# Graph network in four layers on one core: four and five gather buffers, one VectorE increment per group of operations, frames per five chunks

## The chip, the cores and the metric

One core of a Trainium2 chip. The metric is the device time of one execution in microseconds (us), as the median of three runs. Engines: PE is TensorE, DVE is VectorE, ACT is ScalarE, POOL is GpSimd, SP is SyncE. A semaphore is a counter in hardware that instructions increment when they finish and that others wait on.

## The reference

12,500 nodes with 32 features and 400,000 edges, sorted by their target `dst`. Each of four layers gathers the features of the source node of every edge, makes a message of them and of the edge's attributes, adds the messages up by target, and is followed by a residual and a layer norm:

```python
x = _layernorm(x + _L0_gnn_ref(x, edge_index, edge_weight1, edge_attr_3, edge_attr_5, L0_gnn_W), axis=-1)
x = _layernorm(x + _L1_gnn_ref(x, edge_attr_2, L1_gnn_weight, edge_index), axis=-1)
x = _layernorm(x + _L2_gnn_ref(x, edge_index, edge_attr_2, L2_gnn_g, L2_gnn_mu, ...), axis=-1)
x = _layernorm(x + _L3_gnn_ref(x, edge_weight, edge_attr_3, edge_index, ...), axis=-1)
```

The first layer multiplies the gathered, transformed features with products of spherical harmonics `sh0`, `sh1`, `sh2` (one, three and five attributes per edge). The third takes three 32-wide blocks of `x[src] @ g`, weights them with three Gaussians of the edge's two attributes and adds them:

```python
diff = edge_vectors[:, None, :] - mu[None, :, :]
gauss = jnp.exp(-0.5 * jnp.sum(diff * diff / (EPS + sigma[None] ** 2), axis=-1))
msg = jnp.sum((x[src] @ g).reshape(e, k, cout) * gauss[:, :, None], axis=1)
```

## The kernel before, in words

The edges lie on 128 partitions with 3,125 each. An edge stage works in 125 **chunks** of T = 25 edges per partition. For each chunk SyncE loads the source indices and the attributes, GpSimd issues 25 indirect DMAs (each gathers one row per partition from a table in DRAM: 512 bytes in the first layer, 384 in the third), VectorE makes the messages and runs a scan along the edges (the mask from ScalarE restarts it at each new target), and ScalarE turns the scan's result and stores it. After the stage the rows at the ends of the runs are fetched. The first and the third layer use the same frame (`vector_edges`, `scalar_edges`, `gpsimd_edges`, `sync_edges`, with `layer` 0 or 2); layers two and four have code of their own, which stays as it is.

There are three gather buffers, `L.gb[k % 3]`, and each engine runs a hardware loop of 25 bodies of five chunks (BODY = 5). Since five is no multiple of three, a table says which chunk used a buffer last:

```python
BEFORE3 = {0: (3, 1), 1: (4, 1), 2: (2, 1), 3: (0, 0), 4: (1, 0)}
```

Chunk 0 of a body waits for chunk 3 of the body before, that is two chunks back, and chunk 1 for chunk 4, two back as well; chunk 2 waits for the one five back; 3 and 4 for the one three back. SyncE and GpSimd both wait on VectorE's counter `dv` for the last product that reads the buffer (`mk[layer, "g", b_]`), SyncE before it loads the indices (line 2075), GpSimd before its gathers (line 1912).

VectorE increments `dv` with every instruction, 29 times per chunk in the first layer (27 in the body function and 2 for the copy and the scan behind it) and 27 in the third (25 + 2), and `after(e)` (line 392) makes it wait until all its own increments have arrived, ahead of each step that reads what the step before wrote. The first layer's steps per chunk are: five one-hots (L584, for a histogram of the sources on TensorE), three copies (L870 to L872), six small operations (L875 to L879), two more (L881, L882), nine products (L891 to L898), two reductions (L901, L902), a copy (L1164) and the scan (L1169). The third layer's are the direction frames of 25 columns (L913 to L944, stored to `Y_d` for the fourth layer), the Gaussians (L955 to L961), the product (L966), the reduction (L971), and copy and scan. ScalarE takes a square root and an exponential for each chunk (L1391, L1393).

In the first layer SyncE issues six DMAs per chunk: indices (L2075), three attributes (L2078), and two stores that fill scratch areas (L2079, L2080). In the third it issues four: indices, two attributes (L2082, L2085) and the store of the frames (L2089).

## Time and profile before

| | |
|---|---|
| median of 3 runs | 22449.03 us (22440.92 to 22450.41) |
| the profiled execution: span | 22477.8 us; its time outside the span isn't given, and the span lies 28.8 us above the median |
| first layer's edge stage | 170 to 4642 us |
| third layer's edge stage | 11500 to 15920 us |
| busy over the span | PE 33%, PEld 24%, DVE 56%, ACT 16%, POOL 57% |
| busy in the first layer's stage | DVE 2792 us, POOL 2952 us of 4472 us |
| busy in the third layer's stage | DVE 1528 us, POOL 2953 us of 4420 us |

How to read it: GpSimd counts as busy only while it works on an indirect DMA (0.94 us each), not in the 0.30 us between two, so its busy share in a stage without any pause would be some 75%. Waiting instructions and DMA issues aren't busy time. In a row of the timeline the brackets give how long the engine was idle before it, and what ended that; "issue" and "remote" name no instruction.

### The profile page before, as it was taken

To read this page: it belongs to the slowest core of one execution; us is meant where nothing else is said; L and a number is where in the kernel's file an instruction comes from. 1 tells how busy PE (TensorE), PEld (TensorE's weight loads), DVE (VectorE), ACT (ScalarE), POOL (GpSimd) and SP (SyncE) were. 2 spreads that over 40 slices of the span, in tenths; PEclk is the share of its full clock that TensorE was granted. 3 is DMA by queue.
4 is the path that set the end of the run, shared out by engine and by line. 5 is a ranking of instruction groups with operands and counts; after the bars stand their busy time and mean duration, and the time that the engine had idled before them with its cause. 6 is when DMAs were issued, how large, how long until landed. Compare 5 with 4: busy or idle time off the path is not lost. (4 is left out here: it accounts for less than half of the span.)

```text
span 22477.8 us, 146858 instructions
## 1 busy us (share of the span) xinstructions
PE 7373.1 (33%) x33487; PEld 5470.9 (24%) x33487; DVE 12681.8 (56%) x18038; ACT 3608.5 (16%) x5762; POOL 12798.1 (57%) x13715
## 2 busy tenths in 40 slices
PE   1111011114444444444420000000166666666664
PEld 0000000003333333333310000000155555555553
DVE  5666666646666666666753333333366666666665
ACT  0000000001111111111531111111111111111111
POOL 6666666655555555555656666666644444444444
PEclk9755555556666666666755555555588888888887
DMA  3222222210000000000322222222111111111111
GB/s 92 86 86 86 85 83 86 87 34 19 19 18 18 18 19 19 18 18 18 128 90 52 52 52 52 52 52 52 36 38 35 37 35 35 37 35 35 37 35 30
DMA packets 787591, 1077.91 MB, mean 48 GB/s; under 512 B 412503, under 2 KB 554765, under 8 KB 774494
## 3 DMA queue, kind: packets, MB, share of 16 engines
q0 software_dynamic: 417376, 477.82, 9.8%
q1 hardware_dynamic: 294051, 398.16, 6.4%
q10 hardware_dynamic: 75736, 197.70, 2.4%
q14 instruction: 340, 2.79, 0.0%
q8 instruction: 88, 1.44, 0.0%
HBM read 684.92 MB, written 389.48 MB: 48 GB/s over the span
## 5 line engine op out<-in xcount | busy, mean ns | idle before, releaser
L1912 POOL DMA_INDIRECT s_arena<-d_t,s_arena x6250 | 5901.2, 944 | 2983.8 <-issue 2482.7
L1884 POOL DMA_INDIRECT s_arena<-d_t,s_arena x3125 | 2958.8, 947 | 3193.9 <-DVE s_arena L1033 1127.9
L1845 POOL DMA_INDIRECT d_pay<-s_arena x3125 | 3025.9, 968 | 2938.8 <-DVE s_arena L717 1469.3
L1699 PE MATMUL psall<-s_w2r,s_arena 128*128 128x384 f32 x4750 | 2070.4, 572 | 1635.6 <-DVE s_arena L1033 844.5
L1593 PE MATMUL psall<-s_arena 128*128 128x500 bf16 x1875 | 986.3, 553 | 4661.7 <-DVE s_arena L584 2352.5
L1619 PE MATMUL psall<-s_arena 128*128 128x128 f32 x6250 | 1338.7, 377 | 1877.6 <-ACT s_arena L1339 1560.6
L1699 PEld LDWEIGHTS psall<-s_w2r,s_arena 128*128 128x128 f32 x4750 | 1445.0, 319 | 1993.2 <-DVE s_arena L1033 904.9
L1619 PEld LDWEIGHTS psall<-s_arena 128*128 128x128 f32 x6250 | 1149.8, 274 | 2180.6 <-issue 1210.6
L1030 DVE TENSOR_TENSOR s_arena<-psall,s_arena 128x512 f32<-128x512 f32 x1000 | 788.9, 789 | 1554.6 <-remote 1367.5
L1593 PEld LDWEIGHTS psall<-s_arena 128*128 128x128 bf16 x1875 | 219.4, 117 | 5234.3 <-DVE s_arena L584 2495.5
L1785 PE MATMUL psall<-s_tails,s_mfix 128*128 128x32 f32 x6 | 1.9, 411 | 4445.4 <-DVE s_tails L1177 4445.4
L1042 DVE TENSOR_REDUCE s_arena<-s_arena 128x64 f32<-128x1024 f32 x1000 | 1401.5, 1412 | 0.2 <-issue 0.2
L901 DVE TENSOR_REDUCE s_arena<-s_arena 128x600 f32<-128x4200 f32 x125 | 1027.2, 8218 | 552.2 <-remote 519.1
L1507 ACT ACTIVATE s_arena<-s_arena 128x800 f32<-128x800 f32 x250 | 428.8, 1715 | 5470.3 <-issue 3357.9
L1339 ACT ACTIVATE s_arena<-psall 128x512 f32<-128x512 f32 x875 | 482.4, 551 | 4870.9 <-remote 2623.7
L708 DVE TENSOR_TENSOR s_arena<-psall,s_arena 128x512 f32<-128x512 f32 x875 | 551.0, 630 | 1048.8 <-remote 939.2
L1610 PE MATMUL psall<-s_ident,s_arena 128*128 128x128 f32 x3125 | 718.7, 369 | 1274.2 <-DVE s_arena L685 1274.2
L1785 PEld LDWEIGHTS psall<-s_tails,s_mfix 128*128 128x128 f32 x6 | 1.5, 313 | 4446.7 <-DVE s_tails L1177 4446.7
L697 DVE TENSOR_TENSOR s_arena<-s_arena,psall 128x625 f32<-128x625 bf16 x625 | 503.5, 806 | 1008.3 <-remote 706.5
L584 DVE TENSOR_TENSOR s_arena<-s_arena,psall 128x625 bf16<-128x625 f32 x1250 | 944.9, 800 | 0.4 <-DVE s_arena L1151 0.4
L1610 PEld LDWEIGHTS psall<-s_ident,s_arena 128*128 128x128 f32 x3125 | 551.7, 196 | 1297.3 <-issue 1297.3
L685 DVE TENSOR_TENSOR s_arena<-s_arena,psall 128x1536 f32<-128x1536 f32 x250 | 781.6, 3168 | 4.4
(296 smaller groups left out, 16815.9 us busy)
## 6 DMA issues: line engine op xcount, KB each, us to landing
s_arena<-d_t,s_arena POOLq DMA_INDIRECT x9375
d_scan<-s_arena ACTq DMA_DIRECT2D x375, 400.0 KB
s_arena<-d_ew SPq DMA_DIRECT2D x126, 800.0 KB, 6.4
s_arena<-d_pay SPq DMA_DIRECT2D x33, 1650.0 KB, 6.9
d_inj<-s_agg SPq DMA_DIRECT2D x125, 400.0 KB
s_arena<-d_inj SPq DMA_DIRECT2D x125, 400.0 KB
d_pay<-s_arena POOLq DMA_INDIRECT x3125
d_pay<-s_agg SPq DMA_DIRECT2D x100, 429.0 KB
```

Source lines behind the costliest of these rows:

```text
L584: return e.tensor_tensor(O[sl], h5[:, :, bass.ds(n, 1)].to_broadcast([P, 5, 125]), iob, ALU.is_equal)
L685: up(e.tensor_tensor(xb[:, t0:t1], so_[:, t0:t1].unsqueeze(2).to_broadcast([P, t1 - t0, 4, 32]), tv[:, t0:t1].unsqueeze(3).to_broadcast([P ...
L901: e.tensor_reduce(S[:, :, 8:32], w7.rearrange("p m t c -> p t c m"), AX.X, ALU.add).then_inc(dv.up(), 1)
L1030: e.tensor_tensor(pr[:, :, 0:256].rearrange("p t (b v) -> p t b v", v=16), Rg[:, :, 0:256].rearrange("p t (b v) -> p t b v", v=16), L3.G[s ...
L1042: e.tensor_reduce(L3.sums[s2][:, t0:t0 + n].rearrange("p t c -> p (t c)"), prod(g).rearrange("p t (b v) -> p (t b) v", v=16), AX.X, ALU.ad ...
L1593: e.matmul(R5s[:, 0:4], lhsT, rhs[:, 0:4], start=start, stop=True, skip_group_check=True)
L1610: m = e.transpose(ps[6][:, 128 * t:128 * t + 128], S1.xb[:, 128 * (t0 + t):128 * (t0 + t) + 128], ident[:, :])
L1619: m = e.matmul(ps[2 + yb][:, 128 * t:128 * t + 128], S1.xT[yb][:, 128 * t:128 * t + 128], S1.wt, start=True, stop=True)
L1699: m = e.matmul(ps[BANK[g] + t][:, 0:384], hv_[:, :, t0 + t], L3.w2v if g in ONPE else w2r[:, :], start=True, stop=True)
L1845: e.indirect_dma_start(pay_d, bass.IndirectOffsetOnAxis(ap=S1.adr[s4][:, t:t + 1], axis=0), S1.pay[s4][:, 33 * t:33 * t + 33], None).then_ ...
L1884: e.indirect_dma_start(L3.gb[s][:, t], None, T3_d, bass.IndirectOffsetOnAxis(ap=L3.idx[s][:, t:t + 1], axis=0)).then_inc(sem(f"g3_{s}"), 16)
L1912: e.indirect_dma_start(L.gb[s][:, t * L.CW:(t + 1) * L.CW], None, L.tab, bass.IndirectOffsetOnAxis(ap=L.idx[s][:, t:t + 1], axis=0)).then_ ...
```

## The change

*First layer.* Four gather, attribute and index buffers instead of three. Chunk 0 stands ahead of the loop, then 31 bodies of four chunks, so each chunk reuses the buffer of the chunk four before it. VectorE increments `dv` five times per chunk: when the attributes are copied ("ready"), the small operations done ("turned", "oh"), the products done ("g"), the sums done ("S"). It waits on its own count five times. The scan of a chunk comes first in the next chunk. The one-hots come in groups of three and two among the small operations, and TensorE's count of them goes up once per chunk. ScalarE's mask has two PSUM buffers.

*Third layer.* Five gather, index, row and scan buffers, and still bodies of five. VectorE increments `dv` three times per chunk. The frames and the Gaussians are computed for the five chunks of the next body at once (125 columns), in twelve steps of which one is put behind the product, the reduction and the scan of each chunk but the fifth; the first body's are done ahead of the loop. Square root and exponential come once per body. SyncE loads the attributes and stores the frames once per body, and loads each index list five chunks ahead.

The rest of the kernel is the same. The core of the diff (removed functions are in the listing above):

```diff
-BODY = 5
-IT = TP // (T * BODY)
+B2 = 5
+IT2 = TP // (T * B2)
...
-            L.gb = [cv(T * L.CW) for _ in range(3)]
-            L.idx = [cv(T, U32) for _ in range(3)]
...
+        L0.gb = [cv(T * 128) for _ in range(3)]
+        L0.idx = [cv(T, U32) for _ in range(3)]
+        L0.at = [cv(T * 9) for _ in range(3)]
...
+        cv = Carve(21400)
+        L0.gb.append(cv(T * 128))
+        L0.at.append(cv(T * 9))
+        L0.idx.append(cv(T, U32))
...
+        TB = T * B2
+        L2.CW = 96
+        L2.gb = [cv(T * 96) for _ in range(B2)]
+        L2.idx = [cv(T, U32) for _ in range(B2)]
...
+        L2.dirs, L2.at, L2.YS = cv(TB * 3), cv(TB * 2), cv(TB * 9)
+        L2.DF, L2.GS, L2.SQ, L2.n2 = part(cv(TB * 6), 0, 6, TB), part(cv(TB * 3), 0, 3, TB), part(cv(TB * 3), 0, 3, TB), part(cv(TB), 0, 1, TB)
...
+        PER0 = 5
+        AT0 = {"ready": 1, "turned": 2, "oh": 3, "g": 4, "S": 5}
+        def v0(c, name):
+            return c * PER0 + (mk["base0"] + AT0[name])
+        def vector_scan0(e, c, s2):
+            e.wait_ge(dv.h, v0(c, "S"))
+            e.wait_ge(sem("am0"), c + 1)
+            e.wait_ge(sem("rowc0"), c + 1)
+            return e.tensor_tensor_scan(L0.so[s2], mr[s2], L0.si[s2], 0.0, ALU.mult, ALU.add)
...
+        def vector_chunk0(e, c, i, k):
+            s, s2 = k % 4, k % 2
...
+            if i is not None:
+                vector_scan0(e, c - 1, 1 - s2)
+            e.wait_ge(sem(f"at0_{s}"), nth4(0 if i is None else i, k) * 48)
+            e.tensor_copy(a0, tv(0, 1))
+            e.tensor_copy(s1x[:, :, 0:3], tv(1, 3))
+            e.tensor_copy(s1x[:, :, 3:5], tv(1, 3)[:, :, 0:2]).then_inc(dv.up(), 1)
+            e.wait_ge(sem("cnt_pe"), c + 1)
+            for q in range(3):
+                onehot(e, c * 5 + q, q)
+            e.wait_ge(dv.h, v0(c, "ready"))
+            e.tensor_copy(L0.siv[s2][:, :, 0:1], L0.sov[1 - s2][:, :, T:T + 1])
+            e.tensor_scalar(sn, s1x[:, :, 2:5], -1.0, None, ALU.mult)
             for o0, st_, f in ((2, 4, 0), (1, 2, 1), (5, 2, 3)):
...
+                e.tensor_scalar(Q[:, :, o0:o0 + st_ + 1:st_], a2[:, :, f:f + 1].to_broadcast([P, T, 2]), QA, None, ALU.mult)
+            e.tensor_scalar(Q[:, :, 4:5], a2[:, :, 2:3], QC, None, ALU.mult)
             e.tensor_scalar(bm, a2[:, :, 2:3], -QB, None, ALU.mult).then_inc(dv.up(), 1)
...
+            for q in range(3, 5):
+                onehot(e, c * 5 + q, q)
+            e.wait_ge(dv.h, v0(c, "turned"))
+            e.scalar_tensor_tensor(out=Q[:, :, 0:1], in0=a2[:, :, 4:5], scalar=-QA, in1=bm, op0=ALU.mult, op1=ALU.add)
             e.scalar_tensor_tensor(out=Q[:, :, 8:9], in0=a2[:, :, 4:5], scalar=QA, in1=bm, op0=ALU.mult, op1=ALU.add).then_inc(dv.up(), 1)
...
+            e.wait_ge(sem(f"g_{s}"), nth4(0 if i is None else i, k) * 400)
+            e.tensor_tensor(w7[:, 0], A1_, a0.to_broadcast([P, T, 24]), ALU.mult)
+            e.tensor_tensor(wu(1), b3(A2_, 3), bm2(a1, 8), ALU.mult)
+            e.tensor_tensor(wu(2), A4_[:, :, :, 2:5], bm2(s1x[:, :, 1:4], 8), ALU.mult)
+            e.tensor_tensor(wu(3), A4_[:, :, :, 1:4], bm2(sn, 8), ALU.mult)
+            e.tensor_tensor(w4[:, :, :, 0], g0[:, :, 0:8], a0.to_broadcast([P, T, 8]), ALU.mult)
+            e.tensor_tensor(w4[:, :, :, 1:4], A3_, bm2(a1, 8), ALU.mult)
+            e.wait_ge(dv.h, v0(c, "oh"))
             for j in range(3):
...
+                m = e.tensor_tensor(wu(4 + j), A5_[:, :, :, j:j + 1].to_broadcast([P, T, 8, 3]), bm2(Q[:, :, 3 * j:3 * j + 3], 8), ALU.mult)
+            m.then_inc(dv.up(), 1)
+            e.wait_ge(dv.h, v0(c, "g"))
+            e.tensor_reduce(S[:, :, 8:32], w7.rearrange("p m t c -> p t c m"), AX.X, ALU.add)
             e.tensor_reduce(S[:, :, 0:8], w4, AX.X, ALU.add).then_inc(dv.up(), 1)
...
+        PER2L = 3 * B2
+        def of0(k):
+            return (32, 31, 31, 31, 0)[k]
+        def vl2(i, k, n):
+            return i * PER2L + (mk["base2l"] + 3 * k + n)
...
+            if ph == 0:
+                e.wait_ge(sem("dr2"), 16 * step + 16)
+                e.tensor_tensor(SQ, a3, a3, ALU.mult)
+                e.wait_ge(sem("at2"), 16 * step + 16)
+                return e.tensor_tensor(DV, bm2(a2, 3), mug[:, :].rearrange("p (k d) -> p k d", k=3).unsqueeze(1).to_broadcast([P, TB, 3, 2]), ALU.subtract)
+            if ph == 1:
+                e.tensor_tensor(DF, DF, DF, ALU.mult)
+                return e.tensor_reduce(n2, SQ, AX.X, ALU.add)
+            if ph == 2:
+                return e.tensor_tensor(DF, DF, sgg[:, :].unsqueeze(1).to_broadcast([P, TB, 6]), ALU.mult)
+            if ph == 3:
+                return e.tensor_reduce(L2.GS, DV, AX.X, ALU.add)
+            if ph == 4:
+                e.wait_ge(sem("ac_n2"), step + 1)
+                return e.reciprocal(n2, n2)
+            if ph == 5:
+                e.wait_ge(sem("yst"), 16 * step + 16)
+                e.tensor_tensor(n_[:, :, 0:2], a3[:, :, 1:3], n2.to_broadcast([P, TB, 2]), ALU.mult)
+                return e.tensor_tensor(n_[:, :, 2:3], a3[:, :, 0:1], n2, ALU.mult)
+            if ph == 6:
...
+        def vector_chunk2l(e, i, k, last):
...
+            prev = L2.sov[(k - 1) % B2]
+            step = i + 1
+            e.wait_ge(dv.h, vl2(i, k, 0))
+            if k == 0:
+                e.wait_ge(sem("ac_gs"), step)
+            e.wait_ge(sem(f"g_{k}"), i * 400 + (400 + 400 * of0(k)))
+            m = e.tensor_tensor(
+                L2.work.rearrange("p (q c) -> p q c", c=32), g0.rearrange("p t (q c) -> p (t q) c", c=32),
+                L2.GSP[:, k * T:k * T + T].rearrange("p t (q o) -> p (t q) o", o=1).to_broadcast([P, 3 * T, 32]), ALU.mult)
+            if not last and k < 4:
+                m = vector_frames(e, i, 3 * k, step)
+            m.then_inc(dv.up(), 1)
+            e.wait_ge(dv.h, vl2(i, k, 1))
+            e.tensor_copy(L2.siv[:, :, 0:1], prev[:, :, T:T + 1])
+            m = e.tensor_reduce(L2.sit, L2.work.rearrange("p (t q c) -> p t c q", t=T, q=3), AX.X, ALU.add)
+            if not last and k < 4:
+                m = vector_frames(e, i, 3 * k + 1, step)
+            m.then_inc(dv.up(), 1)
+            e.wait_ge(dv.h, vl2(i, k, 2))
+            e.wait_ge(sem("am2"), c + 1)
+            e.wait_ge(sem("rowc2"), c + 1)
+            m = e.tensor_tensor_scan(L2.so[k], mr[0], L2.si, 0.0, ALU.mult, ALU.add)
+            if not last and k < 4:
+                m = vector_frames(e, i, 3 * k + 2, step)
+            m.then_inc(dv.up(), 1)
+        def vector_edges2(e):
+            e.memset(mrv[0][:, :, 0:1], 0.0).then_inc(dv.up(), 1)
...
+            mk["first2l"] = dv.n
+            for ph in range(12):
+                if ph:
+                    after(e)
+                vector_frames(e, 0, ph, 0).then_inc(dv.up(), 1)
+            mk["base2l"] = dv.n
...
+        def scalar_chunk2l(e, i, k, last):
+            c = i * B2 + k
+            e.wait_ge(dv.h, vl2(i, k, 0))
+            scalar_mask(e, c, 0, 2)
+            if not last and k == 1:
+                e.wait_ge(dv.h, vl2(i, 0, 2))
+                e.activation(L2.n2, L2.n2, ACT.Sqrt).then_inc(sem("ac_n2"), 1)
+            if not last and k == 4:
+                e.wait_ge(dv.h, vl2(i, 4, 1))
+                e.activation(L2.GSP, L2.GS, ACT.Exp, scale=-0.5).then_inc(sem("ac_gs"), 1)
+            e.wait_ge(dv.h, vl2(i, k, 3))
+            e.wait_ge(sem(f"rowd2_{k}"), i * 16 + 16)
+            e.activation(L2.row[k].rearrange("p (t f) -> p t f", t=T), L2.sov[k][:, :, 1:T + 1].rearrange("p f t -> p t f"), ACT.Copy).then_inc(sem("rowc2"), 1)
...
+        def gpsimd_chunk0(e, c, i, k):
+            s = k % 4
+            e.wait_ge(sem(f"ix_{s}"), nth4(0 if i is None else i, k) * 16)
+            held(e)
+            e.wait_ge(dv.h, v0(c - 4, "g"))
+            held(e)
+            for t in range(T):
...
+                    e.wait_ge(sem(f"ix_{k}"), i * 16 + (16 + 16 * of0(k)))
...
+                    e.wait_ge(dv.h, vl2(i - 1, k, 1))
...
+        def sync_chunk0(e, c, i, k):
+            s = k % 4
+            e.wait_ge(dv.h, v0(c - 4, "g"))
+            e.sem_inc(idle2, 1)
+            e.dma_start(L0.idx[s].bitcast(I32), src_v[:, bass.ds(c * T, T)]).then_inc(sem(f"ix_{s}"), 16)
+            for o, w_, a_ in ((0, 1, ew1), (1, 3, ea3), (4, 5, ea5)):
+                e.dma_start(L0.at[s][:, o * T:(o + w_) * T], a_.rearrange("(p t) d -> p (t d)", p=P)[:, bass.ds(c * (T * w_), T * w_)]).then_inc(sem(f"at0_{s}"), 16)
+            if i is None:
+                lo_, n = 0, 14
+            else:
+                lo_, n = i * (106 * 33) + (14 + 27 * (k - 1) - (k == 4)) * 33, 26 + (k < 3)
+            e.dma_start(pay_d.rearrange("(p t) c -> p (t c)", p=P)[:, bass.ds(lo_, 33 * n)], agg[:, 0:33 * n]).then_inc(sem("fill_p"), 16)
+            e.dma_start(inj_d[0:E, :].rearrange("(p t) f -> p (t f)", p=P)[:, bass.ds(c * 800, 800)], agg[:, 924:1724]).then_inc(sem("fill_z"), 16)
...
+            with e.Fori(0, IT2 - 2) as i:
+                for k in range(B2):
+                    sync_after2(e, i, k, 1)
+                    sync_index2(e, i + 1, k)
+                    if k == 2:
+                        sync_attr2(e, i + 2)
+                    if k == 4:
+                        e.dma_start(Y_d[:, bass.ds((i + 1) * (TB * 9), TB * 9)], L2.YS).then_inc(sem("yst"), 16)
```

Three places where the order of the instructions changes. VectorE, first layer, in the loop, from the attribute copies on; `m_dv` is its own counter, `m_at0_1` the attributes, `m_cnt_pe` TensorE's count. Before:

```order
L870 COPY psall<-s_arena 128x25 [waits m_at0_1,m_dv]
L871 COPY psall<-s_arena 128x25x3
L872 COPY psall<-s_arena 128x25x2
L392 REGISTER_ALU
L875 TENSOR_SCALAR psall<-psall 128x75 [waits m_dv]
L877 TENSOR_SCALAR psall<-s_arena 128x25x2 x3
L878 TENSOR_SCALAR psall<-s_arena 128x25
L879 TENSOR_SCALAR s_arena<-s_arena 128x25
L392 REGISTER_ALU
L881 SCALAR_TENSOR_TENSOR psall<-s_arena 128x25 [waits m_dv]
L882 SCALAR_TENSOR_TENSOR psall<-s_arena 128x25
L392 REGISTER_ALU
```

After:

```order
L870 COPY s_arena<-s_arena 128x32 [waits m_dv]
L871 TENSOR_SCALAR psall<-psall 128x75
L873 TENSOR_SCALAR psall<-s_arena 128x25x2 x3
L874 TENSOR_SCALAR psall<-s_arena 128x25
L875 TENSOR_SCALAR s_arena<-s_arena 128x25
L564 ISA
L564 TENSOR_TENSOR s_arena<-s_arena,psall 128x5x125
L564 ISA
L564 TENSOR_TENSOR s_arena<-s_arena,psall 128x5x125
L879 REGISTER_ALU
L880 SCALAR_TENSOR_TENSOR psall<-s_arena 128x25 [waits m_dv]
L881 SCALAR_TENSOR_TENSOR psall<-s_arena 128x25
```

Before, every copy, operation and product here carries an increment; in the new order only L875 and L881 do (and L864, the last attribute copy, some rows earlier), and two one-hots stand between the small operations and the wait of L880.

VectorE, third layer, from the Gaussians of a chunk to its scan; `m_g2_1` and `m_g_1` are gathers, `m_ac_gs` and `m_ac_n2` ScalarE's results. Before:

```order
L955 TENSOR_TENSOR s_arena<-s_arena,s_mug 128x150 [waits m_at2_1]
L392 REGISTER_ALU
L957 TENSOR_TENSOR s_arena<-s_arena 128x150 [waits m_dv]
L392 REGISTER_ALU
L959 TENSOR_TENSOR s_arena<-s_arena,s_sgg 128x150 [waits m_dv]
L392 REGISTER_ALU
L961 TENSOR_REDUCE s_arena<-s_arena 128x75 [waits m_dv]
L966 TENSOR_TENSOR s_arena<-s_arena,psall 128x2400 [waits m_g2_1,m_ac_gs]
L392 REGISTER_ALU
L971 TENSOR_REDUCE s_arena<-s_arena 128x25x32 [waits m_dv]
L392 REGISTER_ALU
L1164 COPY s_arena<-s_arena 128x32 [waits m_dv]
```

After:

```order
L992 TENSOR_TENSOR s_arena<-s_arena,psall 128x2400 [waits m_g_1]
L953 TENSOR_REDUCE s_arena<-s_arena 128x375
L999 REGISTER_ALU
L1000 COPY s_arena<-s_arena 128x32 [waits m_dv]
L1001 TENSOR_REDUCE s_arena<-s_arena 128x25x32
L955 REGISTER_ALU
L956 RECIPROCAL s_arena<-s_arena 128x125 [waits m_ac_n2]
L1006 REGISTER_ALU
L1007 REGISTER_ALU [waits m_dv]
L1009 SCALAR_TENSOR_TENSOR s_arena<-psall,s_arena 128x832 [waits m_rowc2,m_am2]
L959 TENSOR_TENSOR s_arena<-s_arena 128x125x2 [waits m_yst]
L960 TENSOR_TENSOR s_arena<-s_arena 128x125
```

The product no longer waits for Gaussians of its own chunk; behind product, reduction and scan one step of the next body's frames stands each time.

SyncE, third layer, one chunk before:

```order
L2075 ISA [waits m_dv]
L2075 DMA s_arena<-in_src 128x25
L2082 ISA
L2082 DMA s_arena<-in_edge_attr 128x50
L2083 REGISTER_ALU
L2085 ISA [waits m_dv]
L2085 DMA s_arena<-in_edge_attr 128x75
L2087 ISA
L2089 ISA [waits m_dv]
L2089 DMA d_y<-s_arena 128x225
```

After, chunks 1 to 3 of a body:

```order
L2158 ISA [waits m_dv]
L2158 DMA s_arena<-in_src 128x25
L2162 REGISTER_ALU
L2158 ISA [waits m_dv]
L2158 DMA s_arena<-in_src 128x25
L2153 ISA
L2153 DMA s_arena<-in_edge_attr 128x250
L2154 ISA
L2154 DMA s_arena<-in_edge_attr 128x375
L2162 REGISTER_ALU
L2158 ISA [waits m_dv]
L2158 DMA s_arena<-in_src 128x25
```

Of four DMAs per chunk one is left, and the attributes of five chunks are loaded together in the body's third chunk.

## Rows read from the trace of the kernel before

**Rows 1.** The page: its first line and its part 1 (busy us, share, instructions).

```profile
span 22477.8 us, 146858 instructions
PE 7373.1 (33%) x33487; PEld 5470.9 (24%) x33487; DVE 12681.8 (56%) x18038; ACT 3608.5 (16%) x5762; POOL 12798.1 (57%) x13715
```

**Rows 2.** Busy time by stage: us, PE, PEld, DVE, ACT, POOL, clock, DMA, GB/s.

```profile
170.00:4642.00 4472.00, 441.31 (x1250) 81.67 (x1250) 2791.96 (x3672) 319.75 (x250) 2952.15 (x3129) 0.58 0.30 85
...
11500.00:15920.00 4420.00, 4.86 (x28) 3.29 (x28) 1528.35 (x3395) 733.23 (x793) 2952.71 (x3125) 0.50 0.22 52
```

**Rows 3.** Line L1912, 170 to 4660 us: duration min/median/max, first and last start.

```profile
L1912 POOL DMA_INDIRECT s_arena<-d_t,s_arena x3125: 938/944/967, 180.0 to 4587.5; - x196
```

**Rows 4.** The same line from 11500 to 16000 us.

```profile
L1912 POOL DMA_INDIRECT s_arena<-d_t,s_arena x3125: 938/944/1172, 11517.0 to 15904.7; - x196
```

**Rows 5.** Timeline of GpSimd, 2069 to 2140 us: start, duration, engine, idle before.

```profile
2108.12 0.94 POOL L1912 DMA_INDIRECT s_arena<-d_t,s_arena  x1 [0.30 <-issue]
2134.66 0.94 POOL L1912 DMA_INDIRECT s_arena<-d_t,s_arena  x1 [25.59 <-DMA s_arena<-in_src]
```

**Rows 6.** VectorE's line groups, 170 to 4660 us: busy, mean ns, idle before.

```profile
L901 DVE TENSOR_REDUCE s_arena<-s_arena 128x600 f32<-128x4200 f32 x125 | 1027.2, 8218 | 552.2 <-remote 519.1 <-issue 29.5 <-DVE s_arena L898 2.8
...
L1169 DVE TENSOR_TENSOR_SCAN s_arena<-psall,s_arena 128x832 f32<-128x832 f32 x125 | 236.3, 1891 | 29.0 <-issue 21.8 <-DVE s_arena L1164 7.2
...
L891 DVE TENSOR_TENSOR s_arena<-s_arena,psall 128x600 f32<-128x600 f32 x125 | 97.5, 780 | 276.7 <-remote 212.3 <-issue 61.4 <-DVE psall L882 1.9
...
L875 DVE TENSOR_SCALAR psall<-psall 128x75 f32<-128x75 f32 x125 | 30.6, 245 | 183.1 <-remote 127.4 <-issue 52.0 <-DVE psall L872 2.2
...
L881 DVE SCALAR_TENSOR_TENSOR psall<-s_arena 128x25 f32<-128x25 f32 x125 | 25.8, 206 | 611.0 <-remote 479.9 <-issue 130.2
```

**Rows 7.** Timeline of all engines, 2042 to 2066 us.

```profile
2042.36 0.20 DVE L881 SCALAR_TENSOR_TENSOR psall<-s_arena 128x25 f32<-128x25 f32 x1 [6.93 <-remote]
...
2045.16 0.78 DVE L891 TENSOR_TENSOR s_arena<-s_arena,psall 128x600 f32<-128x600 f32 x1 [2.49 <-remote]
2045.81 0.70 SPq L2079 DMA_DIRECT2D d_pay<-s_agg  x1
...
2050.33 0.77 DVE L898 TENSOR_TENSOR s_arena<-s_arena,psall 128x600 f32<-128x600 f32 x1
...
2057.06 8.22 DVE L901 TENSOR_REDUCE s_arena<-s_arena 128x600 f32<-128x4200 f32 x1 [5.96 <-remote]
```

**Rows 8.** Timeline of VectorE, the first layer's last chunk.

```profile
4618.11 3.64 DVE L584 TENSOR_TENSOR s_arena<-s_arena,psall 128x625 bf16<-128x625 f32 x5
...
4623.40 0.78 DVE L891 TENSOR_TENSOR s_arena<-s_arena,psall 128x600 f32<-128x600 f32 x1
...
4629.38 8.22 DVE L901 TENSOR_REDUCE s_arena<-s_arena 128x600 f32<-128x4200 f32 x1
...
4638.91 1.89 DVE L1169 TENSOR_TENSOR_SCAN s_arena<-psall,s_arena 128x832 f32<-128x832 f32 x1 [0.19 <-DVE s_arena L1164]
```

**Rows 9.** VectorE's line groups, 11500 to 16000 us.

```profile
L966 DVE TENSOR_TENSOR s_arena<-s_arena,psall 128x2400 f32<-128x2400 f32 x125 | 332.0, 2656 | 626.9 <-DMA s_arena<-d_t,s_arena 534.2 <-ACT psall L1393 79.4 <-issue 13.2
...
L957 DVE TENSOR_TENSOR s_arena<-s_arena 128x150 f32<-128x150 f32 x125 | 39.6, 317 | 845.6 <-remote 575.1 <-issue 267.7 <-DVE s_arena L955 2.5
```

**Rows 10.** Timeline of all engines, 176 to 186 us.

```profile
177.15 0.40 SPq L2075 DMA_DIRECT2D s_arena<-in_src  x1
...
180.03 0.95 POOL L1912 DMA_INDIRECT s_arena<-d_t,s_arena  x1 [5.47 <-DMA s_arena<-in_src]
...
184.90 0.08 DVE L557 MEMSET s_cst<- 128x1 f32 x4
```

**Rows 11.** Timeline of all engines, 15880 to 15935 us.

```profile
15907.26 2.66 DVE L966 TENSOR_TENSOR s_arena<-s_arena,psall 128x2400 f32<-128x2400 f32 x1 [1.97 <-DMA s_arena<-d_t,s_arena]
```

**Rows 12.** SyncE's waits, 170 to 4660 us: total us, times, longest.

```profile
SPq L2074 <- remote: 1024.0, 44, 55.3
SPq L2074 <- DVE s_arena L898: 330.3, 8, 49.8
```

503 lines of the change are left out of this document (208 added, 295 removed).

## The prediction

> **What bounds the kernel now.** I read the page first, then each engine's busy time by stage, then the queue of gathers, then VectorE's line groups and a piece of the timeline. On the page no engine is busy for more than 57% of the span [rows 1], so the limit differs by stage. The change touches two: the first layer's edge loop (170 to 4642 us) and the third layer's (11500 to 15920 us), each 125 chunks of 25 gathers [rows 2]. The other 13,400 us run the same instructions as before, and I cost them at nothing.
>
> In the first layer the gathers start at 180.0 us and the last of the 3,125 at 4587.5 us [rows 3]; in the third from 11517.0 to 15904.7 us [rows 4]. A gather takes 0.94 us and the next starts 0.30 us behind it, and then one comes after 25.59 us, behind an index load [rows 5]. I took the step between every two neighbours. In the first layer the median is 1.249 us, no step inside a chunk is over 1.273 us, and the excess over 3,124 equal steps is 4407.5 - 3902 = 505 us, nearly all of it in the 24 steps where a body of five ends (21.7 us each). In the third it is 4387.7 - 3902 = 486 us, spread over most chunk boundaries (4 to 9 us). So GpSimd's queue has a floor of 3902 us in each stage, and something makes it wait for 991 us in all.
>
> What it waits for is VectorE. In the first layer VectorE is busy 2792 us [rows 2], 22.3 us per chunk, and idle 552 + 611 + 277 + 183 = 1623 us before four lines [rows 6]: together 4415 of the 4461 us. It is never starved of data there (except for the first chunk); it waits for its own increments. The group L891 to L898, nine instructions with an increment each, ends at 2051.1, but L901, which needs the ninth, starts at 2057.06; meanwhile SyncE's DMA issues take 0.70 us each instead of the 0.40 us of the stage's first [rows 7, 10]. From L891 to L901 that is 11.9 us for nine increments, 1.3 us each; L881 and L882, two increments, take 2.8 us. In the last chunk, when SyncE and the gathers are through, the same nine instructions take 5.98 us and the whole chunk, 4618.11 to 4640.80, takes 22.7 us [rows 8]. So beside SyncE's work an increment costs up to 1.4 us, and the 29 of a chunk lengthen it from 22.7 us to 35.7 in the mean (4461 / 125).
>
> With three buffers and a body of five, chunk 0 of a body reuses buffer 0, last used two chunks earlier instead of three. There GpSimd has to wait for the slow VectorE, then for SyncE, then for the index load; this is the 21.7 us. The third layer has the same arrangement and 27 increments per chunk, with much longer waits in its chain of small operations [rows 9].
>
> **The change, part by part.** *Buffers.* With four buffers and bodies of four (five and five), every chunk waits for the one four (five) before it. That leaves at least three chunks of gathers, 94 us, for one chunk of VectorE and one of SyncE, so if VectorE needs under 31.2 us per chunk (25 x 1.249), GpSimd never waits.
>
> *Increments, first layer.* 29 per chunk become 5. The chunk keeps its operations and so its 22.3 us of busy time. VectorE waits for itself five times; at the worst seen, 1.4 us behind a single increment, that is 7 us, so 22.3 to 29.3 us. Two of the waits stand behind three and two one-hots (0.73 us each), and the wait for "oh" behind six products, so I take two exposed waits: 22.3 + 2.8 = 25.1 us. All of it is below 31.2 us, so it costs nothing on the path. **Term 1: -505 us.**
>
> *The end of the first layer.* Today VectorE is behind: from the start of the last gather to the end of the last scan 4640.8 - 4587.5 = 53.3 us pass. Afterwards it is idle when the last gather lands. The third layer shows that distance now: 15904.7 to L966 at 15907.26, 2.6 us [rows 11]. Then come 17.4 us from L891 to the end of the scan [rows 8], and up to two waits of 1.4 us (I take one): 21.4 us. **Term 2: -32 us.**
>
> *The start of the first layer.* SyncE's first index load now waits for VectorE's count to reach 16 below its value at the loop. Before it was 33 below, passed at 176.9 us; counted back along the instructions, 16 below falls on the last of the four memsets of L557, at 185.0 us [rows 10]. The first gather, at 180.03, follows. **Term 3: +8 us.**
>
> *Third layer.* 27 increments become 3 per chunk. The direction and Gaussian work is done once per five chunks on 125 columns instead of 25, spread over twelve of the fifteen steps of a body. VectorE's 12.2 us per chunk (1528 / 125 [rows 2]) can only shrink, since fewer instructions move the same elements; with three waits of 1.4 us it is under 17 us. ScalarE's square root and exponential come once per body. The first body's twelve steps run before VectorE's first product, while the first 31 us of gathers run; even at two waits each they delay no buffer among five. **Term 4: -486 us**, and one memset less ahead of the barrier, -0.8 us. The tail stays: already now VectorE waits for the last gather there.
>
> *SyncE.* In the first layer it waits 1024 + 330 us for VectorE's count [rows 12], so it works some 3,100 us, 24.8 us per chunk, beside those increments. Six DMAs per chunk stay, with 24 increments fewer to compete with: 24.8 us is the upper bound and below 31.2. In the third layer, eight DMAs per body replace twenty. The larger loads and the larger Y store (128x1125) lie more than a chunk ahead of their use. Cost nothing; without that cover a body would pay one load, 2 to 3 us.
>
> *GpSimd.* Same gathers. A step of 1.249 us is the sum's main price. Its bounds are rows of busy time: 938 ns at least and 1172 ns at most, against a median of 944 [rows 4].
>
> Here a rule speaks against the change. What the row shows is L901 starting 5.96 us behind nine increments, and no wait in the last chunk [rows 7, 8]. The Trainium skill, VectorE: DVE Perf Modes, section "The DRAIN you can't avoid", says that eight copies with a semaphore after each took the same time as with one only after the last, and its rules say to minimize the count of operations, not of semaphores. By that rule the last chunk agrees and the middle of the stage does not; if it held, term 1 would be zero. 
>
> **Sum:** -505 - 32 + 8 - 486 - 1 = -1016 us against a span of 22477.8. The page gives no other time of this execution than its span, which is 28.8 us above the median of the runs, 22449.0; I subtract from the median: **21433 us**, 4.5% faster.
>
> **The rivals.**
> *B: the waits do not follow the number of increments.* If VectorE's 13.2 us of waiting per chunk (1652 / 125, the four lines and the scan's 29 us [rows 6]) stayed in the first layer, a chunk would be 35.5 us and VectorE would set the pace: terms 1 and 2 are lost. 22449 + 8 - 487 = 21970 us. For it: a wait is also two register instructions. Against: 2, 6 and 9 increments wait 2.5, 6.9 and 6.0 us behind their instructions. If instead each exposed wait cost 3.3 us, the present mean (1652 / 500), a chunk would be 31 to 33 us, and the time up to 21433 + 125 x 1.8 = 21660 us. Chance 0.06 for both.
> *C: GpSimd still pauses at some body boundaries*, because SyncE comes to an index load late behind its fills. A mean of a quarter of today's pause per body, 5.4 us x 31, and half the third layer's excess: +167 + 243 = 21840 us. Against: the slack of several chunks. Chance 0.05.
> *D, slower: the gathers themselves slow down.* GpSimd now pauses 11% of both stages; without pauses, and with VectorE's work no longer broken up by waits, each gather would have to exceed (4407.5 + 4387.7) / 6248 = 1.408 us for the kernel to lose. If each took the longest seen, 1172 instead of 944 ns, the step would be 1.477 us: 6248 x 0.069 = +431 us, less the 25 us of terms 2 and 3: 22855 us. Against: inside the first layer's chunks no step moves by 2% while VectorE is busy 62% of the time, and in the third 99 of 100 steps are below 1.303 us. The Trainium skill, SBUF — State Buffer, section on the doors into SBUF ("The 'DVE blocks DMA' trap"), has such a mechanism: a 2-port copy on VectorE keeps GpSimd from writing descriptors. By that rule copies should show as late gathers; in this trace they do not. Chance 0.03.
> *E: no difference* (within 0.2%, 45 us, about what a measurement of this kernel can tell): the gains and a partial D cancel. Chance 0.02.
>
> **How the numbers follow.** The forecast has 0.84. Its own range: a step of 1.244 us, the smallest seen, would give 31 us more; five exposed waits change only the tail, by 4 us; a load exposed once per body would cost 56 bodies x 2.5 = 140 us. So 21400 to 21570; the mild form of B lies half inside it. A fifth or less is left out, so it is the range of the whole. The forecast, B and C are all faster: faster 0.95, same 0.02, slower 0.03.
>
> **What would show it.** Gathers of the first layer from 188 to 4090 us, with no pause over 2 us; those of the third spanning 3902 us; steps of 1.249 us. VectorE idle in both stages ahead of the first product (L890, L992), waiting for a gather, and at most 1.4 us ahead of the reductions; its first-layer busy time still near 2790 us, in the third below 1528. SyncE waiting more than before. The first layer's last scan some 21 us behind the last gather. The prediction is wrong if VectorE's idle time in the first layer lies before the reductions instead (B), if pauses of GpSimd follow an index load (C), or if its step is above 1.26 us (D).

## The result, and the profile after

| | before | after |
|---|---|---|
| median of 5 runs | 22450.41 us (22440.92 to 22453.89) | 22371.12 us (22360.98 to 22384.42) |
| ratio, 95% interval | | 0.9965, 0.9955 to 0.9976 |
| span of the profiled execution | 22477.8 us | 22369.0 us |

The change is worth 79 us (0.35%), not 1016; the time is 801 us above the range's upper end. Three views answer to [rows 1 to 4]: the page's first part; the two stages by windows (us, then PE, PEld, DVE, ACT, POOL busy, clock, DMA share, GB/s); the two lines of gathers (duration ns min/median/max, first to last start):

```profile
PE 7326.9 (33%) x33487; PEld 5554.2 (25%) x33487; DVE 12331.2 (55%) x15713; ACT 3280.0 (15%) x5336; POOL 13220.2 (59%) x13715
```

```profile
170.00:4642.00 4472.00, 350.77 (x1250) 144.16 (x1250) 2787.07 (x3669) 317.63 (x249) 2995.38 (x3128) 0.54 0.30 85
11430.00:15820.00 4390.00, 14.76 (x95) 10.27 (x91) 1192.29 (x1098) 411.02 (x402) 3321.54 (x3126) 0.50 0.22 53
```

```profile
L1957 POOL DMA_INDIRECT s_arena<-d_t,s_arena x3125: 938/945/1803, 202.2 to 4570.8; - x196
...
L1979 POOL DMA_INDIRECT s_arena<-d_t,s_arena x3125: 940/946/2245, 11454.7 to 15800.7; - x196
```

From first to last start, the gathers take 4368.6 us in the first layer and 4346.0 us in the third, against 4407.5 and 4387.7 before: 81 us less instead of 991.

The two layers miss 3902 us in different ways, which the starts of the gathers show. In the first layer GpSimd still pauses: 56 steps, all at the start of a chunk, are longer than 3.2 us, and they hold 417 of the 467 us over 3902; the steps inside chunks hold 48. In the third it never pauses so long, but its busy time rose from 2953 to 3322 us: 1208 of 3124 steps are longer than 1.3 us, 731 of them between 1.38 and 1.42.

Not all of the 79 us need come from the two loops that were changed. In this pair of traces the first layer gives nothing to the total: its gathers start 22.2 us later, its last scan comes 72.7 us behind its last gather instead of 53.3, and the second layer's gathers start at 4971.7 us against 4968.9. The second layer's gathers, whose code is the same, take 5856.0 us against 5918.1, which is 62 of the 109 us between the spans; the pair on one chip below has no such difference.

VectorE's line groups of the first layer (busy, mean ns, idle before) answer to [rows 6]:

```profile
L901 DVE TENSOR_REDUCE s_arena<-s_arena 128x600 f32<-128x4200 f32 x125 | 1027.2, 8218 | 775.5 <-remote 678.6 <-issue 96.2
L564 DVE TENSOR_TENSOR s_arena<-s_arena,psall 128x625 bf16<-128x625 f32 x625 | 473.6, 803 | 132.8 <-issue 132.4
L898 DVE TENSOR_TENSOR s_arena<-s_arena,psall 128x600 f32<-128x600 f32 x375 | 284.6, 775 | 203.1 <-issue 170.9 <-remote 32.1
...
L890 DVE TENSOR_TENSOR s_arena<-s_arena,psall 128x600 f32<-128x600 f32 x125 | 96.1, 769 | 41.4 <-DMA s_arena<-d_t,s_arena 41.4
...
L880 DVE SCALAR_TENSOR_TENSOR psall<-s_arena 128x25 f32<-128x25 f32 x125 | 25.4, 203 | 467.9 <-remote 418.5 <-issue 49.4
```

Before L901, L564, L898 and L880 VectorE waits 1579 us, against 1652 before the change. Before the first product (L890), where I expected the waits, it is only 41.4 us, in three waits. So in the first layer VectorE almost never runs out of gathered rows: it is busy 22.3 us of a chunk, waits 12.6 (1579 / 125), and with these 35 us it sets the pace, while GpSimd pauses. In VectorE's timeline the nine products run one behind the other, with one increment behind the last, and the reduction still starts 5.51 us late [rows 7]:

```profile
2062.91 2.14 DVE L898 TENSOR_TENSOR s_arena<-s_arena,psall 128x600 f32<-128x600 f32 x3
2070.56 8.22 DVE L901 TENSOR_REDUCE s_arena<-s_arena 128x600 f32<-128x4200 f32 x1 [5.51 <-remote]
```

### The profile page after: what moved, and what is told of

Same layout as the page of the kernel before. It is cut to its first block and busy times, and to the rows that moved or that the text cites. A ratio compares the mean times of both kernels' runs of the same rounds, so it can differ in the third digit from the quotient of the medians.

```text
span 22369.0 us, 139122 instructions
## 1 busy us (share of the span) xinstructions
PE 7326.9 (33%) x33487; PEld 5554.2 (25%) x33487; DVE 12331.2 (55%) x15713; ACT 3280.0 (15%) x5336; POOL 13220.2 (59%) x13715
## 5 line engine op out<-in xcount | busy, mean ns | idle before, releaser
L1939 POOL DMA_INDIRECT s_arena<-d_t,s_arena x3125 | 2963.9, 948 | 3178.4 <-DVE s_arena L1091 1107.9
L1979 POOL DMA_INDIRECT s_arena<-d_t,s_arena x3125 | 3320.8, 1063 | 1106.6 <-issue 1026.1
L1957 POOL DMA_INDIRECT s_arena<-d_t,s_arena x3125 | 2993.1, 958 | 1405.8 <-issue 1373.3
L992 DVE TENSOR_TENSOR s_arena<-s_arena,psall 128x2400 f32<-128x2400 f32 x125 | 332.0, 2656 | 3141.9 <-DMA s_arena<-d_t,s_arena 3141.9
L901 DVE TENSOR_REDUCE s_arena<-s_arena 128x600 f32<-128x4200 f32 x125 | 1027.2, 8218 | 775.5 <-remote 678.6
L564 DVE TENSOR_TENSOR s_arena<-s_arena,psall 128x625 bf16<-128x625 f32 x1250 | 962.7, 801 | 132.8 <-issue 132.4
```

The lines of the kernel that those rows point to most:

```text
L564: return e.tensor_tensor(O[sl], h5[:, :, bass.ds(n, 1)].to_broadcast([P, 5, 125]), iob, ALU.is_equal)
L901: e.tensor_reduce(S[:, :, 8:32], w7.rearrange("p m t c -> p t c m"), AX.X, ALU.add)
L1939: e.indirect_dma_start(L3.gb[s][:, t], None, T3_d, bass.IndirectOffsetOnAxis(ap=L3.idx[s][:, t:t + 1], axis=0)).then_inc(sem(f"g3_{s}"), 16)
L1957: e.indirect_dma_start(L0.gb[s][:, t * 128:(t + 1) * 128], None, T0_d, bass.IndirectOffsetOnAxis(ap=L0.idx[s][:, t:t + 1], axis=0)).then_i ...
L1979: e.indirect_dma_start(L2.gb[k][:, t * 96:(t + 1) * 96], None, T2_d, bass.IndirectOffsetOnAxis(ap=L2.idx[k][:, t:t + 1], axis=0)).then_inc ...
```

## The experiments

**Increments, and the engine that issues.** inc29 gives the 28 instructions of a first-layer chunk (all but the scan, which carries none in either) their increment back:

```diff
-        PER0 = 5
-        AT0 = {"ready": 1, "turned": 2, "oh": 3, "g": 4, "S": 5}
+        PER0 = 28
+        AT0 = {"ready": 3, "turned": 13, "oh": 17, "g": 26, "S": 28}
-            e.tensor_copy(a0, tv(0, 1))
+            e.tensor_copy(a0, tv(0, 1)).then_inc(dv.up(), 1)
...
```

> The changed kernel with an increment behind every one of the 28 VectorE instructions of a first-layer chunk again, instead of 5; buffers, order and waits stay. By the prediction's own view (a wait grows with the increments) the chunk, now 35 us, can only get longer: 23 increments more at up to 1.4 us each, so the first layer's gathers last more than 4369 us, up to 7000. By the theory that I take now (the wait grows with the instructions and goes by SyncE's issues, increments or not) nothing changes: 4369 us within 1%, and VectorE still idle some 1600 us there.

Measured: 22364.47 us (one run; before on the same chip 22430.36), the first layer's gathers in 4369.6 us. Going from 5 increments to 28 changes nothing here: not the stage, and not the wait before the first reduction (504.7 us from 1000 to 3800 us, against 505.1 in after). The Trainium skill, VectorE: DVE Perf Modes, section "The DRAIN you can't avoid", says that a semaphore behind each of eight copies cost nothing extra. This run, with other instructions than copies, agrees with that rule, which the prediction had set aside.

fills_act moves the fill stores into ScalarE's loop, loads_act the index and attribute loads too (three chunks ahead), third_act the third layer's index loads and Y stores:

```diff
 # fills_act, in scalar_edges0 (and out of sync_chunk0)
                     scalar_row0(e, c, i, k - 1, 1 - k % 2)
+                    scalar_fill0(e, c, i, k)
 # loads_act: besides
+                    load0(e, c + 3, (k + 3) % 4)
 # third_act, in scalar_chunk2l
+            if not last:
+                sync_index2(e, i + 1, k)
```

> The changed kernel with the first layer's two fill stores per chunk issued by ScalarE instead of SyncE. Same bytes, same number of DMAs. If VectorE's waits come from SyncE's issuing (six DMAs per chunk, now four), they shrink by about a third: 1650 to some 1100 us, a chunk of 31 us or less, and the gathers end 350 to 460 us earlier. If they come from the bytes that the DMA queues move, or from the gathers alone, the stage stays at 4369 us.

> As the run before it, and the first layer's index and attribute loads on ScalarE too: SyncE issues nothing there after the first four chunks. If SyncE's issuing makes VectorE wait, VectorE's chunk falls to the 22 to 25 us of the last chunk and GpSimd sets the pace: gathers of the first layer in 3902 us (-465), 21905 us in all. If the gathers alone make it wait, the stage stays near 4369 us.

> The changed kernel with the third layer's index loads and Y stores issued by ScalarE instead of SyncE, which keeps two loads per body of five. Theory: a gather that takes 1.09 us instead of 0.94 does so because SyncE's instructions want the same path. Then nearly all of the 443 us of slow steps go: third layer's gathers 3902 to 3960 us instead of 4346, 21950 us in all. Rival: the other queues' bytes in flight slow the gathers. They are the same bytes, so the stage stays at 4346 us.

Measured: 22388.55, 22387.91 and 22372.67 us, one run each (before on the same chip 22430.36). Gathers of the first layer 4374.5 us (fills_act) and 4383.6 (loads_act), of the third 4345.9 (third_act). The changed kernel itself wasn't run on this chip, but each of these runs leaves one stage as it is: 4368.9 us in third_act's first layer, 4346.1 in fills_act's third. So SyncE's issuing is not the cause. In loads_act SyncE is silent after four chunks, ScalarE's instructions take 0.70 us, and from 1000 to 3800 us VectorE waits 516.5 us before L901, against 505.1 in after.
**Packets and bytes.** latefill takes the fills out of the loop and issues them behind it; thinfill puts two 128 x 25 stores in their place; idx_one loads a body's indices at once; dup adds three index loads per chunk:

```diff
 # latefill
+            fills0(e, 0, None, 0)
+            with e.Fori(0, 31) as i:
+                for k in range(1, 5):
+                    fills0(e, i * 4 + k, i, k)
             e.wait_ge(sem("fill_p"), 125 * 16)
 # idx_one
+            e.dma_start(L2.ib[b].bitcast(I32), src_v[:, bass.ds(i * TB, TB)]).then_inc(sem(f"ix_{b}"), 16)
 # dup
+                    for d_ in L2.dup:
+                        e.dma_start(d_.bitcast(I32), src_v[:, bass.ds(i * TB + k * T, T)]).then_inc(sem("dup"), 16)
```

> The changed kernel with the first layer's fill stores taken out of its loop and issued by SyncE in one row behind it, so that the loop has 5 queue DMAs per chunk instead of 7 and 702 packets beside the gathers instead of 990. Theory R, formed from the traces: with 7 such DMAs per chunk every engine but GpSimd goes at 0.70 us an instruction for some 27 us of a chunk's 35; that is 27 ns a packet, and VectorE's waiting (13.4 us a chunk) goes by the packets. Then it falls to 9.5 us, the chunk to 32 us, the gathers of the first layer from 4369 to some 4000 us; the fills cost their own time behind it. If the waiting comes from VectorE and the gathers alone, 4369 us stay.

> As the run before it, but two thin stores of 128 x 25 elements per chunk stand in the loop in place of the fills: the same 990 packets per chunk, 3% of the fills' bytes. If the number of packets counts, the first layer's gathers last 4369 us as in the changed kernel; if the bytes count, some 4000 us as in the run before.

> The changed kernel with the third layer's five index loads of a body merged into one of 128 x 125: 4 of 13 queue DMAs per body less, 254 packets per chunk beside the gathers instead of 369. Theory R: the slow gathers' excess (443 us) goes by these packets and falls to 305 us, gathers in 4210 us instead of 4346. If it goes by VectorE's or ScalarE's activity, nothing changes.

> The changed kernel with three more index loads per chunk in the third layer, into buffers that nothing reads: 801 packets per chunk beside the gathers instead of 369. Theory R: excess 443 x 801/369 = 960 us, gathers in 4860 us; by SyncE's instructions alone it would be as much, but moving them to ScalarE changed nothing. Rival: bytes or VectorE set it, 4346 us.

These four fell on a chip where the kernel before takes 17400.39 us, 5000 less: 17575.96, 17575.34, 17420.36 and 17417.37 us. I call it chip B, the others chips A. The gathers of latefill, and VectorE's waits from 1000 to 3800 us:

```profile
L1957 POOL DMA_INDIRECT s_arena<-d_t,s_arena x3125: 940/944/966, 203.8 to 4103.7; - x196
...
L1979 POOL DMA_INDIRECT s_arena<-d_t,s_arena x3125: 940/944/1170, 9212.1 to 13123.2; - x196
```

```profile
L901 DVE TENSOR_REDUCE s_arena<-s_arena 128x600 f32<-128x4200 f32 x89 | 731.3, 8217 | 3.0
...
L890 DVE TENSOR_TENSOR s_arena<-s_arena,psall 128x600 f32<-128x600 f32 x90 | 70.2, 780 | 833.1 <-DMA s_arena<-d_t,s_arena 833.1
```

This is the prediction's picture of after: 3899.9 and 3911.1 us, no pause, VectorE waiting almost only for gathers. But there the kernel before is as short: 17400 us against 17417 with the change and three idle loads more (one run each). With 991 us of pauses it would be longer, so the pauses that the change was to remove can't be there; no trace of the kernel before on chip B shows it directly.

So I ran both kernels again on one chip:

> The changed kernel itself again, beside the kernel before. In the last four runs both lasted 17400 to 17580 us instead of 22370 to 22450, on another chip. If a run is of that kind again: theory, there the gathers go at 1.249 us without pauses in all four gather stages of either kernel (each 3902 us and up), the change removes nothing but a few waits, and the ratio is within 0.2% of 1. Rival: the kernel before still pauses there at its body boundaries as the prediction has it, and the changed one is up to 1016 us faster. If it is of the first kind, 22371 us and a ratio of 0.9965.

> The kernel before, for its profile on the same chip. On a chip of the second kind: every step of a gather 1.249 us, VectorE waiting for gathers in all stages, SyncE's instructions at 0.03 to 0.05 us instead of 0.70. On one of the first kind the trace is that shown of before, 22478 us.

It was a chip A: 22644.38 against 22729.29 us, ratio 0.9964, interval 0.9951 to 0.9978. The gathers of before_again (two lines), then of after_again:

```profile
L1912 POOL DMA_INDIRECT s_arena<-d_t,s_arena x3125: 941/947/988, 178.5 to 4622.4; - x196
...
L1912 POOL DMA_INDIRECT s_arena<-d_t,s_arena x3125: 941/947/1266, 11577.8 to 15970.7; - x196
```

```profile
L1957 POOL DMA_INDIRECT s_arena<-d_t,s_arena x3125: 938/944/1803, 203.9 to 4597.3; - x196
...
L1979 POOL DMA_INDIRECT s_arena<-d_t,s_arena x3125: 940/945/2247, 11557.8 to 15907.8; - x196
```

On one chip the spans differ by 22723.9 - 22653.0 = 70.9 us. The third layer's gathers last 42.9 us less. The first layer's end 25.1 us earlier, but 10.9 of these are lost in its longer tail (below), and the second layer's gathers start 14.3 us earlier. The other 14 us lie in parts that the change leaves as they are.

Then the four once more, again on a chip A (before 22622.60 us):

> The kernel of latefill, on a chip of the first kind if it falls on one (22400 us for the kernel before). Theory R as there: 5 queue DMAs and 702 packets per chunk beside the gathers instead of 7 and 990, VectorE's waiting by the packets 9.5 us a chunk instead of 13.4, gathers of the first layer in some 4000 us instead of 4369; the fills behind the loop took 158 us on the other chip, so 210 us faster than the changed kernel in all. Rival: waiting by VectorE's own instructions, 4369 us stay and it is 158 us slower.

> As latefill_b, with the two thin stores per chunk in the fills' place: packets as in the changed kernel, 3% of the fills' bytes. If packets count: gathers in 4369 us; if bytes: some 4000 us.

> The kernel of dup on a chip of the first kind: 801 packets per third-layer chunk beside the gathers instead of 369. Theory R: gathers of that layer in 4860 us instead of 4346. Rival (bytes, or the instructions of VectorE): 4346 us. On a chip of the other kind 3913 us, as there.

> The kernel of idx_one on a chip of the first kind: 254 packets per third-layer chunk beside the gathers instead of 369. Theory R: gathers in 4210 us instead of 4346. Rival: 4346 us.

| run | total, us | first layer, us | third layer, us |
|---|---|---|---|
| latefill_b | 22746.04 | 4393.3 | 4346.4 |
| thinfill_b | 22728.59 | 4389.9 | 4346.4 |
| dup_b | 22520.66 | 4382.2 | 4346.5 |
| idx_one_b | 22526.46 | 4377.5 | 4346.1 |

latefill_b is slower than before (1.0051, interval 1.0033 to 1.0069). Theory R falls. In the first layer 29% fewer packets leave 4393 us (dup_b and idx_one_b, which change nothing there, have 4382 and 4378); in the third 31% fewer or 117% more leave 4346. latefill_b loses what its fills cost behind the loop. What stands out is that on chips A the third layer's gathers last 4346 to 4350 us in every version so far. Taking them 125 at a time, I found in after 156.8 us, 166.3, and then 175.0 for each of the 22 that follow; dup_b and third_act agree within 0.3 us. 175.0 / 125 is 1.400 us. That suggested a ceiling of the gathers themselves, and the last three runs test it:

```diff
 # both20, both10 (n = 20, 10), first and third layer
-            for t in range(T):
+            for t in range(n):
 # alone, in gpsimd_edges2 ahead of the loop
+            with e.Fori(1, 12) as j:
+                for k in range(B2):
+                    e.wait_ge(sem(f"ga_{k}"), j * 400)
+                    held(e)
+                    for t in range(T):
+                        e.indirect_dma_start(...)
```

> The changed kernel with 20 gathers per chunk instead of 25 in the first and third layers (from the sixth chunk on; the last 5 columns of a buffer keep older rows, so the layers' results are left out of the question). Theory G, from the traces so far: on a chip of the first kind a gather costs 1.400 us in the long run, and short steps of 1.249 us only use up a reserve; VectorE's waits are a consequence. Then a chunk takes 20 x 1.400 = 28.0 us in both layers, 3.5 ms a layer. Rival V: VectorE (first layer) and the other queues (third) set 35 us by themselves, and the chunk stays at 35.0. Rival S: the step is 1.249 and the rest is fixed: 25.0 + 3.8 = 28.8 in the third. On a chip of the other kind: 25.0 us.

> As the run before it with 10 gathers per chunk. Theory G: 14.0 us of gathers per chunk, so VectorE sets the first layer's pace with next to no waits, 22.7 to 24 us per chunk; its waits of 13 us come from the gathers' backlog. Rival V: 35 us per chunk in the first layer. Third layer by G: 14.0 us per chunk, or what VectorE and ScalarE need if that is more.

> The changed kernel with 60 chunks of the third layer's gathers (1500, the first body's indices each time, a gather buffer reused after five chunks) ahead of that layer's loop, while every other engine stands at its barrier or waits: the gathers by themselves. Theory G: after a reserve of 7 to 9 chunks the step is 1.400 us, 175 us per five chunks. Rival: alone they go at 1.249 us throughout, 156 us per five chunks, and only the work of other engines or queues makes them slower. On a chip of the other kind: 1.249 us.

Windows of 1400 us in the third layer: after, both20, both10 and alone, one fence each; the number behind POOL's busy time counts its instructions, and its line group there has 1001 gathers in all four.

```profile
12000.00:13400.00 1400.00, 0.00 (x0) 0.00 (x0) 378.95 (x337) 129.03 (x112) 1069.39 (x1001) 0.50 0.22 52
```

```profile
12000.00:13400.00 1400.00, 0.00 (x0) 0.00 (x0) 470.37 (x420) 161.24 (x140) 1055.28 (x1001) 0.50 0.23 57
```

```profile
10200.00:11600.00 1400.00, 0.00 (x0) 0.00 (x0) 942.03 (x841) 322.50 (x280) 1078.63 (x1001) 0.50 0.29 78
```

```profile
12000.00:13400.00 1400.00, 0.00 (x0) 0.00 (x0) 0.00 (x0) 0.00 (x0) 1090.57 (x1001) 0.50 0.17 35
```

A gather costs 1.400 us, whether VectorE is busy for 0, 27, 34 or 67% of the time, and with every other engine idle. In alone the layer's own 3125 gathers follow on without a rest and take 4370.4 us: the short start isn't given a second time. The same window of the kernel before has 995; one of dup on chip B (9500 to 10900 us) has 1118:

```profile
12000.00:13400.00 1400.00, 0.00 (x0) 0.00 (x0) 486.75 (x1077) 233.63 (x248) 939.41 (x995) 0.50 0.22 52
```

```profile
9500.00:10900.00 1400.00, 0.00 (x0) 0.00 (x0) 418.90 (x375) 145.09 (x126) 1059.57 (x1118) 0.50 0.25 60
```

In the third layer rivals V and S are out: with 20 gathers a chunk takes 28.0 us, not 35.0 or 28.8, and alone reaches 1.400 by itself. The Trainium skill, SBUF — State Buffer ("The 'DVE blocks DMA' trap"), blames a VectorE copy for late descriptors; in alone no VectorE instruction runs, so that is not what makes the step 1.400.

In the first layer, from 1000 us on, the window and the line group of L901 in it, both20 then both10:

```profile
1000.00:3500.00 2500.00, 244.12 (x870) 100.33 (x870) 1919.37 (x2524) 222.33 (x174) 1647.67 (x1746) 0.52 0.32 94
```

```profile
L901 DVE TENSOR_REDUCE s_arena<-s_arena 128x600 f32<-128x4200 f32 x88 | 723.1, 8218 | 305.7 <-remote 292.1 <-issue 9.8 <-DVE s_arena L898 2.7
```

```profile
1000.00:2800.00 1800.00, 230.11 (x820) 94.51 (x820) 1791.08 (x2379) 209.54 (x164) 779.53 (x824) 0.52 0.30 94
```

```profile
L901 DVE TENSOR_REDUCE s_arena<-s_arena 128x600 f32<-128x4200 f32 x83 | 682.0, 8217 | 2.8
```

With 10 gathers per chunk VectorE is busy for 1791 of 1800 us, a chunk takes 21.8 us, and the wait before L901 is gone. With 20 the wait is 305.7 / 88 = 3.5 us a chunk, a chunk takes 28.6 us and a gather 2500 / 1746 = 1.432 us; with 25 the wait was 6.2 us. The total times (20770.83, 18218.58 and 24483.18 us, before 22443.65, one run each) follow the number of gathers. So the size of VectorE's waits depends on how many gathers run beside it, and rival V's fixed 35 us is out.

But these waits are also what sets the pace of the first layer. In both20 VectorE never waits for gathers (the first line: L890 from 1000 to 3500 us), while GpSimd waits for the index load of a chunk (the second: its waits in the same stretch), which SyncE issues only when VectorE has freed the buffer:

```profile
L890 DVE TENSOR_TENSOR s_arena<-s_arena,psall 128x600 f32<-128x600 f32 x87 | 67.0, 770 | 0.0
```

```profile
POOL s_arena L1961 <- DMA s_arena<-in_src: 295.3, 33, 11.9
```

Theory G said 28.0 us a chunk for this layer. The measured 28.6 is nearer to what rival S gives if it is carried over from the third layer (28.8), and none of the blocks of 125 gathers of the first layer settle at 175.0 us as the third layer's do: in after they go from 170 to 193, the first two aside. So the ceiling of 1.400 us is shown for the third layer's gathers of 384 bytes. For the first layer's of 512 bytes it is not; they were never run alone.

## Why the prediction was wrong

Two steps failed, one for each layer; terms 1 and 4 rest on them.

*The step that failed in the third layer (term 4, -486)* is "A step of 1.249 us is the sum's main price", with its bounds from rows of duration. 1.249 us is how often a gather can be issued for a while, not what the stage sustains on these chips. The first 125 gathers come at nearly that pace (156.8 us), the next at 1.33 in the mean, and from then on the price is 1.400. Sustained over 3125 that is 4374 us, and the short start gives back 28: 4346. The kernel before stood at 4387.7, so of its 486 us of pauses only 42 were to be had. The pauses did go, and came back as longer gathers: -42.9 us on one chip. The rows hinted at it: in the whole stage a step was 1.405 us (1.411 in the first layer), and every run of 1.249 stood between two pauses [rows 3 to 5].

*The step that failed in the first layer (term 1, -505)* is the sum of the increments, "22.3 + 2.8 = 25.1 us", of which the prediction said that it "costs nothing on the path". "it waits for its own increments", 1.3 us each, is refuted by inc29: 28 increments or 5, the stage stays at 4369 us. VectorE's busy time was right (22.3 us), its waits are 12.6 us a chunk instead of 2.8, and at 35.0 us instead of 25.1 it keeps the pace at which GpSimd has to pause: -50.5 us on one chip, of which the longer tail takes back 10.9. On chip B VectorE has next to no such waits and the stage takes the 3900 us that were forecast. What makes the waits is open; the runs show that it isn't the increments, SyncE's issuing or the packets, and that with fewer gathers they shrink.

*Term 2* (-32) rests on VectorE idling when the last gather comes. On the chip of the pair it is up to three chunks behind with four buffers (VectorE's timeline of after_again, whose last gather starts at 4597.3):

```profile
4595.54 1.89 DVE L847 TENSOR_TENSOR_SCAN s_arena<-psall,s_arena 128x832 f32<-128x832 f32 x1
...
4617.33 1.89 DVE L847 TENSOR_TENSOR_SCAN s_arena<-psall,s_arena 128x832 f32<-128x832 f32 x1
...
4639.11 1.89 DVE L847 TENSOR_TENSOR_SCAN s_arena<-psall,s_arena 128x832 f32<-128x832 f32 x1
...
4660.90 1.89 DVE L847 TENSOR_TENSOR_SCAN s_arena<-psall,s_arena 128x832 f32<-128x832 f32 x1
```

The tail is 65.5 us, before_again's 54.6 (72.7 and 53.3 in the first pair). With the gathers done, a chunk takes 21.8 us, just under the 22.3 of the increments' step.

*Term 3* (+8) was +25 on one chip (+22 in the first pair). The index load went out when I said, but behind ScalarE's copies of the edge weights, which it had preceded before (177.15 us [rows 10]). The copy in before, then after_again:

```profile
179.91 53.96 ACTq L1286 DMA_DIRECT2D d_ew<-in_edge_weight  x1
```

```profile
178.88 51.02 ACTq L1309 DMA_DIRECT2D d_ew<-in_edge_weight  x1
...
183.71 0.37 SPq L2133 DMA_DIRECT2D s_arena<-in_src  x1
...
203.91 0.94 POOL L1957 DMA_INDIRECT s_arena<-d_t,s_arena  x1 [30.26 <-DMA s_arena<-in_src]
```

It took 20 us to land instead of 2.9. I had counted when the load is issued, not what goes out ahead of it. That the copies are what delays it is likely by the order, but no run moves them.

*The rivals.* B has the first layer right, with a chance of 0.06: the waits don't follow the number of increments, and VectorE keeps the pace, at 35.0 us a chunk (B said 35.5). It is wrong in letting the third layer gain its 486 us, so its 21,970 us came out 401 too low. D named the right place in the third layer with a chance of 0.03: gathers without pauses get slower, with a break-even of 1.408 us for both layers; the mean steps came to 1.398 and 1.391. I dismissed it because no step inside a chunk moved, which is what a kernel that pauses before it runs into the ceiling must show.

*Smaller slips.* The stages that the change leaves alone make 13,586 us, not 13,400. The smallest step is 1.242 us, not 1.244. "99 of 100 steps are below 1.303 us" in the third layer holds inside the chunks only. None of them moves the sum.

## What to carry to other kernels

A pause is worth removing only if the queue can keep its short step without it. Divide the stage's time by the number of its gathers first. If a long run without pauses is nowhere in the trace, the mean step, not the median, is the safer price, and the shortest experiment is the queue alone for some hundred instructions. A wait that sits behind many increments isn't shown to come from them until their number is changed with everything else kept. And waits of several engines that grow together suggest something shared.
